# Setup of a fused attention and ternary FFN kernel: k turned, two FFN up blocks, and low parts of weights moved into tile 0

## The reference, cut to what matters

```python
h = x + cosformer_attn(rmsnorm(x, norm1_w), qkv_w, qkv_b, out_w, out_b)   # relu(q), relu(k), causal, 16 heads of 16
return h + gelu(rmsnorm(h, norm2_w) @ mlp_w1 + mlp_b1) @ mlp_w2 + mlp_b2

scale = clip(mean(abs(w_latent), axis=1), 1e-05)                          # bitlinear, for w_fc and w_proj
tern = clip(round(w_latent / scale), -1, 1)
h = bitlinear(x, w_fc) + gate * (x @ v.T @ fast_b.T @ u.T)
return bitlinear(relu(h) ** 2, w_proj)
```

## Time and profile before

| what | value |
|---|---|
| median of three runs | 607.0 us |
| the profiled execution's own time | 607.54 us |
| its span | 605.1 us |
| PE busy | 589.5 us, 97% |
| DVE busy | 395.8 us, 65% |
| ACT busy | 365.1 us, 60% |
| POOL busy | 226.6 us, 37% |

### The profile page before, as it was taken

How to read it: one execution, slowest core, us unless ns; L and a number is a source line. 1 busy time by engine, 2 the same in 40 slices (tenths; PEclk the granted TensorE clock), 3 DMA queues, 4 the chain that set the end, 5 groups by cost and what they waited for, 6 DMA issues and landing times.

```text
span 605.1 us, 14558 instructions
## 1 busy us (share of the span) xinstructions
PE 589.5 (97%) x5162; PEld 525.3 (87%) x5162; DVE 395.8 (65%) x757; ACT 365.1 (60%) x656; POOL 226.6 (37%) x267
## 2 busy tenths in 40 slices
PE   7979999999999999999999999999999999999996
PEld 7868888998898898988899988998989988999785
DVE  6998783685648674585846856486745858457532
ACT  6775774567546765567645675466755676456642
POOL 6446414372144612453142721436124531426220
PEclk9999999999999999999999999999999999999999
DMA  7851026300461007500263004610065002620001
GB/s 222 265 173 53 3 74 115 92 20 2 118 119 42 17 0 155 122 0 17 61 127 89 17 0 117 123 38 17 0 151 127 0 17 54 131 59 2 2 1 35
DMA packets 28009, 42.02 MB, mean 69 GB/s; under 512 B 9024, under 2 KB 19920, under 8 KB 27984
## 3 DMA queue, kind: packets, MB, share of 16 engines
q1 hardware_dynamic: 26800, 39.59, 27.9%
q10 hardware_dynamic: 672, 1.05, 0.6%
q0 software_dynamic: 512, 1.05, 0.6%
HBM read 12.31 MB, written 4.19 MB: 27 GB/s over the span
## 4 chain that ended last, share of the span: by engine, by line
PE 91%; DVE 4%; ACT 3%; issue 1%; POOL 0%; DVEq 0%; POOLq 0%
PE accum L1286 25%; PE dense L1271 10%; PE dense L1454 9%; PE shared L1309 6%; PE ctx_ps L1334 5%; PE dense L1459 5%; PE dense L1321 4%; PE dense L1172 4%; PE shared L1427 3%; PE shared L1186 3%; PE ctx_ps L1345 2%; PE dense L1276 2%; PE dense L1176 2%; PE upd_ps L1359 2%; PE ctx_ps L1203 1%; PE accum L1374 1%
## 5 line engine op out<-in xcount | busy, mean ns | idle before, releaser
L1017 DVE TENSOR_TENSOR wide_lo<-wide,wide_hi 128x512 fp32r<-128x512 f32 x128 | 89.5, 699 | 117.6 <-ACT wide_hi L713 100.4
L1025 DVE TENSOR_TENSOR weighted<-shared,cst 128x512 f32<-128x512 f32 x128 | 82.9, 684 | 18.2 <-PE shared L1309 18.2
L710 ACT ACTIVATE wide<-dense,b 128x512 f32<-128x512 f32 x64 | 44.0, 688 | 83.2 <-PE dense L1459 82.8
L1286 PE MATMUL accum<-w_hi,wide_hi 128*128 128x256 f32 x256 | 72.9, 285 | 2.1 <-DVE wide_lo L1017 2.1
L554 POOL TENSOR_TENSOR state<-state,added 128x544 f32<-128x544 f32 x32 | 43.5, 1359 | 81.1 <-DVE added L1047 80.8
L1286 PE MATMUL accum<-w_lo,wide_hi 128*128 128x256 f32 x256 | 71.9, 281 | 0.0
L1286 PE MATMUL accum<-w_hi,wide_lo 128*128 128x256 f32 x256 | 71.6, 280 | 0.0
L1286 PE MATMUL accum<-prT,wide_hi 128*128 128x256 f32 x256 | 66.8, 289 | 0.6 <-DVE wide_lo L1017 0.6
L1286 PE MATMUL accum<-prT,wide_lo 128*128 128x256 f32 x256 | 65.3, 283 | 0.0
L700 ACT ACTIVATE wide<-dense,scales 128x512 f32<-128x512 f32 x64 | 43.9, 686 | 31.6 <-PE dense L1276 31.3
L571 POOL TENSOR_TENSOR xb<-xb,late 128x512 f32<-128x512 f32 x16 | 20.6, 1290 | 110.5 <-DVE wide_lo L1017 110.5
(11 more groups left out here) (178 smaller groups left out, 1496.1 us busy)
## 6 DMA issues: line engine op xcount, KB each, us to landing
k_stack<-weighted SPq DMA_DIRECT2D x96, 128.0 KB, 2.7
q_stack<-arena SPq DMA_DIRECT2D x176, 64.0 KB, 2.3
xin<-L_attn_x SPq DMA_DIRECT2D x16, 256.0 KB, 2.8
out<-late SPq DMA_DIRECT2D x16, 256.0 KB, 2.2
tab<-trig SPq DMA_DIRECT2D x8, 258.0 KB, 2.7
arena<-L_ffn_w_fc SPq DMA_DIRECT2D x1, 1024.0 KB, 7.6
late<-L_ffn_w_proj SPq DMA_DIRECT2D x1, 1024.0 KB, 7.6
xs<-L_attn_mlp_w SPq DMA_DIRECT2D x2, 512.0 KB, 6.4
```

Source lines behind the costliest of these rows:

```text
L710: act.activation(wide[:, m % 2, :], dense[m % 2][:, :], ACT.Gelu_apprx_tanh, bias=b1[:, m:m + 1]).then_inc(dense_free, 1)
L1017: dve.tensor_tensor(wide_lo[:, n % 2, :], wide[:, n % 2, :], wide_hi[:, n % 2, :].bitcast(F32), ALU.subtract).then_inc(lo_done, 1)
L1025: dve.tensor_tensor(weighted[:, g, :].rearrange("p (a n) -> p a n", a=4), shared[g % 2][:, :].rearrange("p (a n) -> p a n", a=4), mask.rea ...
L1286: mm = pe.matmul(accum[k // 2][:, (k % 2) * E:(k % 2 + 1) * E], a[:, n % 2, tok], w[:, n % HB, :], start=(first and i == 0 and k % 2 == 0) ...
```

## The change

In the setup ACT makes the high parts of k and q as soon as each block is there, and DVE only the low parts; w_fc becomes ternary in two halves, each behind its own scale columns; `wo` is loaded ahead of w_fc and split earlier; ACT instead of DVE makes `diag_scale`. On PE the turn of k, the scale product, FFN up blocks 0 and 1 stand between the turns of u and of w_proj, the latter goes block by block into `accum0`, `accum1`, `ctx_ps` and `upd_ps`, and two of three `keep_busy` are gone. The low parts of w1 and the layernorm go behind the first score groups of tile 0, the w2 quarters to other places in it, and the second half of w1 to the middle of ACT's list. Stacking in tile 0 is issued and waited for by halves (groups 0 and 1, then 2 and 3); POOL starts its part once the high parts of q are there.

The diff, cut:

```diff
-KEEP = (8, 4, 8)
+KEEP = 8
...
+        def wait_k_stack(eng, t, i):
+
+            eng.wait_ge(k_stacked[i], (t + 1) * N_K_STACK // 2 * 16)
+
+        def wait_q_lo(eng, t, i):
+
+            eng.wait_ge(q_lo_stacked[i], (t + 1) * N_Q_LO // 2 * 16)
...
+            sp.dma_start(raw_wo, out_w.rearrange("(k p) n -> p k n", p=P)).then_inc(in_wo, 16)
             sp.dma_start(raw_fc, w_fc.rearrange("(m p) n -> p m n", p=P)).then_inc(in_fc, 16)
-            sp.dma_start(raw_wo, out_w.rearrange("(k p) n -> p k n", p=P)).then_inc(in_wo, 16)
...
-                for g in range(4):
+                def stack_k(g):
                     for slot, part in enumerate((0, 0, 1)):
                         sp.dma_start(k_stack[slot:P:4, g, :, :].bitcast(F32),
-                                     k_parts[32 * g:32 * g + 32, part, :, :]).then_inc(k_stacked, 16)
-                sp.wait_ge(q_parts_done, (t + 1) * 2 * KE)
-                for g in range(4):
-                    stack_q(sp, g, 1, 1, q_lo_stacked)
-                if not isinstance(t, int) or t:
+                                     k_parts[32 * g:32 * g + 32, part, :, :]).then_inc(k_stacked[g // 2], 16)
+
+                if isinstance(t, int) and t == 0:
+                    for i in range(2):
+                        stack_k(2 * i)
+                        stack_k(2 * i + 1)
+                        if i == 0:
+                            sp.wait_ge(q_parts_done, 2 * KE)
+                        stack_q(sp, 2 * i, 1, 1, q_lo_stacked[i])
+                        stack_q(sp, 2 * i + 1, 1, 1, q_lo_stacked[i])
...
-            pool.wait_ge(q_parts_done, 2 * KE)
+            pool.wait_ge(q_hi_made, KE)
...
-                    if isinstance(t, int) and t == 0 and j == 0:
+                    if first and j == 1:
                         pool.wait_ge(in_small, 16 * N_SMALL)
                         pool.wait_ge(w1_lo_done, KE)
-                        pool.wait_ge(lo_done, 2)
                         for g in range(2):
                             x_plus_b2(0, g)
-                    if 1 <= j <= 2:
+                    if first and j >= 2:
+                        xn_plus_ob(j - 1)
+                    elif not first and 1 <= j <= 2:
...
+            def k_hi(m):
+                act.wait_ge(dense_free, m + 1)
+                act.activation(k_parts[:, 0, m, :].bitcast(F32R), kT[:, m, :], ACT.Copy).then_inc(k_hi_made, 1)
+
+            def q_hi(m):
+                act.wait_ge(dense_free, KE + m + 1)
+                act.activation(q_parts[:, 0, m, :].bitcast(F32R), qT[:, m, :], ACT.Copy).then_inc(q_hi_made, 1)
+
+            for m in range(4):
                 sum_abs_fc(m)
             act.wait_ge(in_qkb, 16)
             relu_block(0, 0)
-            for m in range(HB // 2, HB):
-                sum_abs_fc(m)
-            for i in range(1, 2 * KE):
-                relu_block(0, i)
+            k_hi(0)
+            sum_abs_fc(4)
+            sum_abs_fc(5)
+            relu_block(0, 1)
+            k_hi(1)
+            sum_abs_fc(6)
+            sum_abs_fc(7)
+            relu_block(0, 2)
             act.wait_ge(qkv_split, 3 * KE)
-            for m in range(KE):
-                act.wait_ge(dense_free, KE + m + 1)
-                act.activation(q_parts[:, 0, m, :].bitcast(F32R), qT[:, m, :], ACT.Copy).then_inc(q_hi_made, 1)
+            q_hi(0)
+            relu_block(0, 3)
+            q_hi(1)
...
-            act.dma_start(raw_w1[1], mlp_w1[P:2 * P, :]).then_inc(in_w1[1], 16)
-            w1_hi_half(0)
-            read(SET_SC, pr_scale_row[:, :], ctx_ps[:, 0:E])
-            for g in range(4):
-                read(SET_PR + g, prT[:, 2 * g:2 * g + 2, :].rearrange("p h n -> p (h n)"), (accum + dense)[g][:, :])
-            w1_hi_half(1)
-
-            act.wait_ge(set_pe, SET_ALL)
-            act.dma_start(raw_w2[0], mlp_w2[0:4 * P, :].rearrange("(k p) n -> p k n", p=P)).then_inc(in_w2, 16)
+            act.wait_ge(set_dve, N_SET_PR)
+            act.wait_ge(in_const, 16)
+            for m in range(KE):
+                act.activation(diag_scale[:, m, :], ident, ACT.Copy,
+                               scale=scales[:, HB + m:HB + m + 1]).then_inc(diag_done, 1)
...
                 if first:
+                    read_k(0)
+                    read_k(1)
+                    read(SET_SC, pr_scale_row[:, :], ctx_ps[:, 0:E])
+                    act.dma_start(raw_w1[1], mlp_w1[P:2 * P, :]).then_inc(in_w1[1], 16)
+                    w1_hi_half(0)
+                    ffn_block(0)
+                    for g, bank in enumerate((accum[0], accum[1], ctx_ps, upd_ps)):
+                        read(SET_PR + g, prT[:, 2 * g:2 * g + 2, :].rearrange("p h n -> p (h n)"), bank[:, :])
+                    act.dma_start(raw_w2[0], mlp_w2[0:4 * P, :].rearrange("(k p) n -> p k n", p=P)).then_inc(in_w2, 16)
+                    ffn_block(1)
+                    ready_v()
...
+                    if first and j == 0:
+                        w1_hi_half(1)
...
+            split_weight(raw_wo, in_wo, wo_hi, wo_lo, wo_split)
...
-            k_part(0, 0)
-            n = scale_columns(n, 0, HB, E)
-            dve.reciprocal(g_by_s[:, :], scales[:, 0:HB]).then_inc(set_dve, 1)
-            n += 1
-            dve.wait_ge(set_dve, n)
...
+            def fc_half(g, n, between):
+
+                dve.wait_ge(set_dve, n)
+                fc_less(4 * g)
+                for m in range(4 * g, 4 * g + 4):
+                    if m < 4 * g + 3:
+                        fc_less(m + 1)
+                    n += 1
+                    fc_ternary(m, n)
+                    if m == between:
+                        k_low_part(1)
+                return n
+
+            n = scale_columns(n, 0, HB // 2, E)
+            k_low_part(0)
+            n = fc_half(0, n, 1)
+            q_low_part(0)
+            n = scale_columns(n, HB // 2, HB, E)
+            dve.reciprocal(g_by_s[:, :], scales[:, 0:HB]).then_inc(set_dve, 1)
+            n += 1
+            q_low_part(1)
+            n = fc_half(1, n, None)
...
-                dve.tensor_scalar(both, raw_pr[:, m, :], half_neg[:, c:c + 1], None, ALU.is_lt).then_inc(set_dve, 1)
-                dve.tensor_scalar(diag_scale[:, m, :], ident, scales[:, c:c + 1], None, ALU.mult).then_inc(diag_done, 1)
+                dve.tensor_scalar(pr_less, raw_pr[:, m, :], half_neg[:, c:c + 1], None, ALU.is_lt).then_inc(set_dve, 1)
...
-            n = pr_ternary(1, n)
             for g in range(2):
                 dve.wait_ge(read_out, SET_G + g + 1)
                 part = gT[32:64, g * TOK:(g + 1) * TOK]
                 dve.tensor_tensor(part, dense[g][32:64, :], part.bitcast(F32), ALU.subtract).then_inc(g_lo_done, 1)
             z_lo(0)
+            n = pr_ternary(1, n)
...
-            w1_lo_half(0)
-            dve.wait_ge(wo_split, 2)
-            layernorm(0)
-            w1_lo_half(1)
-            dve.wait_ge(read_out, SET_SC + 1)
...
+                first = isinstance(t, int) and t == 0
+                if first:
+                    split(0)
+                for i in range(2):
+                    wait_k_stack(dve, t, i)
                 weigh(0, 0)
-                split(0)
+                if not first:
+                    split(0)
                 weigh(0, 1)
                 for j in range(NB):
                     if j:
                         context(j - 1)
                     weigh(j, 2)
                     weigh(j, 3)
-                    if isinstance(t, int) and t == 0:
-                        w2_quarter((j + 2) % 4, j)
-                    first = isinstance(t, int) and t == 0
+                    if first and j < 2:
+                        w1_lo_half(j)
+                    if first and j == 0:
+                        dve.wait_ge(pr_tern, KE)
...
+                        layernorm(0)
                     if first and j == 2:
+                        w2_quarter(2, 0)
+                        w2_quarter(3, 1)
+                    if first and j == 3:
                         ln_statistics(t + 1, range(2))
-                    if more and j == (3 if first else 0):
+                    if more and j == 0 and not first:
                         sum_halves(t + 1)
                     split(j + 1)
-                    if first and j == 2:
+                    if first and j == 3:
                         ln_statistics(t + 1, range(2, NB))
+                        sum_halves(t + 1)
...
+                if first:
+                    w2_quarter(0, 2)
...
+                if first:
+                    w2_quarter(1, 3)
...
-                keep_busy(KEEP[g])
+                if g == 0:
+                    keep_busy(KEEP)
             pe.wait_ge(u4_done, 1)
-            pe.wait_ge(read_out, SET_FC + 4)
             for g in range(2):
+                pe.wait_ge(read_out, SET_FC + 2 * g + 1)
                 for i in range(4):
                     mm = pe.transpose(dense[g][:, i * P:(i + 1) * P],
```

(46 more changed lines are left out.)

115 lines of the change are left out of this document (63 added, 52 removed).

## The result

The changed kernel takes 610.27 us (median of six runs, 609.58 to 611.94) against 606.65 us for the kernel before in runs beside it. The ratio is 1.0062, 95% interval 1.0045 to 1.0078: it is **slower by 0.6%**, where 602.1 us was forecast, and the range (600.9 to 605.0) missed it. The profiled execution took 610.13 us, its span is 607.7 us, 2.6 more than before.

What follows compares the result with a forecast made beforehand. PE bounds the kernel from tile 1 on, so time saved ahead of the first full chunk is saved at the end. 5.2 gained by chunk 1's group 2, less 0.3, is 4.9; 607.0 - 4.9 = 602.1 us, range 600.9 to 605.0.

Steps and rivals of the forecast that it cites:

- DVE and PE up to the first scores: Setup: u scaled at 25.8 instead of 26.66, first scores at 34.4 instead of 38.60.
- DVE up to the first weigh: Tile 0, chunk 0: DVE free for split at 34.7, weigh follows at 35.3 instead of 40.95.
- The new wait: PE ahead of group 2's scores, for ACT's prT reads and second-half stacks: start at 37.2, bounds 36.6 and 38.7.
- SP issues for the same 13.8: SP's 20 stacking DMAs in tile 0: start 0.3 later, issue for 13.8 us as before, until 33.5.
- The Trainium skill's rule: Stacking DMAs: all issuers share 16 engines, so POOL's earlier start brings no byte forward; sum 4.1 instead of 4.9.
- DVE behind the wait: Chunk 0 from group 2: 7.15 us of DVE work, so chunk 1's group 2 at 44.35, 5.2 us earlier.
- A low clock here is mostly covered: Chunk 0 behind group 2: PE needs 5.3 of the 7.15 and waits for DVE, mostly covering a low clock.
- Chunks 1 to 3: Tile 0: chunk 1's DVE work of 5.6 to 6.0 covered by PE's 5.87; chunk 2's two w2 quarters taken at nothing.
- End of tile 0: A w2 quarter of 1.1 ahead of k and q parts, against DVE's 0.74 idle: PE loses 0.3.
- the first: Rival: second half of the stacks lands late, group 2 at 38.7, 1.5 later: 603.6 us; chance 0.18.
- The second: Rival: ACT becomes the bound, its chain slips by 2.8, prT read at 40: 604.9 us; chance 0.09.
- The third: Rival: PE's clock stays low from group 2 through chunk 1, costing 9.4: 611.5 us; chance 0.06.

Runs made afterwards that it cites:

- 12: Run 9 with low q stacks of groups 2 and 3 on POOL and the last w2 quarter ahead of split 6: 603.64 us, ratio 0.9924 to 0.9962.
- run 10: Run 7 with POOL instead of SP stacking the low parts of q of groups 2 and 3: 605.77 us, ratio 0.9970 to 0.9995.
- run 1: The changed kernel with POOL again waiting for all parts of q before stacking: 609.34 us, ratio 1.0032 to 1.0078.
- run 2: The changed kernel with SP stacking all of k first, then the low parts of q: 609.24 us, ratio 1.0024 to 1.0059.
- run 4: The changed kernel with POOL late, k stacked first and the w2 load held, all together: 610.58 us, ratio 1.0046 to 1.0089.
- 13: Run 11 with SP stacking all of k first, then the low parts of q: 608.01 us, ratio 1.0002 to 1.0030.
- run 11: Run 9 with the last w2 quarter moved ahead of split 6: 604.10 us, ratio 0.9937 to 0.9968.
- 14: Run 11 with POOL waiting for all parts of q before stacking: 604.47 us, ratio 0.9948 to 0.9972.
- run 3: The changed kernel with the load of w2's first half issued behind the v products: 607.60 us, ratio 0.9996 to 1.0024.
- run 5: Run 3 with the load of w1's second half also moved behind the v products: 609.94 us, ratio 1.0036 to 1.0075.
- 8: Run 3 with 24 unread matmuls on PE in its wait for the second half of the stacks: 610.05 us, ratio 1.0035 to 1.0078.
- run 9: Run 7 with 10 unread matmuls on PE in its wait for the stacks: 604.52 us, ratio 0.9947 to 0.9974.
- run 7: Run 3 with POOL's two long operations held until DVE has made both w2 quarters of chunk 2: 606.44 us, ratio 0.9974 to 0.9998.
- run 16: The kernel before with 9 unread matmuls on PE in its wait for the first weigh: 606.86 us, ratio 0.9987 to 1.0012.
- run 6: Run 3 with the two w2 quarters of chunk 2 set one in chunk 2, one in chunk 3: 607.86 us, ratio 1.0001 to 1.0025.

## Why the prediction was wrong, step by step

- *DVE and PE up to the first scores*: right. u at 26.29 (25.8 forecast), the first ternary block at 28.17 (28.0), first scores at 34.49 (34.4). `wo` came in time.
- ***DVE up to the first weigh* failed in its last step.** `split` at 34.95 was as forecast (34.7), but `weigh` did not follow at 35.3: it waited 4.70 us for the stacks of k and started at 40.33. The prediction counted DVE's own work and not the buffer that `weigh` shares with the parts of k. The new order puts the k stacks of groups 2 and 3 behind the low parts of q of groups 0 and 1, and with that this bound alone would have held group 2 back to about 41.2 (an estimate: 40.33 and the 0.8 to 0.9 us by which group 2 follows in runs 12 and 10).
- ***The new wait* failed.** It put group 2 at 37.2, at most 38.7; it started at 41.91, released by the last landing of q, 4.1 later than in the kernel before (37.74 to 41.83).
  1. "SP issues for the same 13.8": 17.9. I carried the sum of a queue over to another order and another neighbour. From 26 to 30 us the engines moved 192 GB/s, 197 with POOL late, 229 with k first, 253 with both and w2 held (runs 1, 2, 4), 265 before. But the landing did not follow these figures: with k first it came 0.4 earlier (run 2) or 1.2 later (13 against 11), with POOL late 0.3 earlier (1) or 0.6 later (14 against 11), all within the scatter. So no run shows what made SP's queue longer.
  2. The w2 load, not in the sum at all: 2.2 us of the landing (run 3), 1.9 over all runs. The prediction counted the 512 KB load that starts later than before, w1, which cost nothing that shows (run 5), and overlooked the one that now starts earlier, at 34.78 instead of 36.27, ahead of the tail and not behind it.
  3. SP starts at 20.21, 0.8 later instead of 0.3.

  The w2 load and the later start are 3.0 of the 4.1 at most; the rest, 1.1 or more, stays open. With the load held, k first and POOL late together (run 4) the landing was still 1.5 behind the kernel before, at a start of SP 0.6 later. In the kernel before the landing (37.74) had 0.9 us to spare ahead of the first scores (38.60), and DVE's work held group 2 back to 41.68 anyway; the change used up both.
- *The Trainium skill's rule*, weighed there, that another issuer brings no byte forward: run 1 agrees, as far as its 0.5 us of POOL's start goes (group 2 0.3 us earlier without the early start, not later). The sum by it, 4.1, missed as mine did, since neither held the w2 load.
- *DVE behind the wait*, 7.15: measured 7.77 at the low clock and 6.29 at the full one (runs 8 and 9). The term that was too large is the layernorm, 1.3 from start to start in the changed kernel (45.79 to 47.08) and not 2.2: before, POOL worked beside it. "A low clock here is mostly covered" was wrong by 1.5 us here, and by 1.1 in run 3 and 2.0 in run 7. What it costs in the kernel before is open (run 16).
- *Chunks 1 to 3*, "taken at nothing": chunk 1 right (5.87 from 49.68 to 55.55), chunk 2 lost 1.56 (a wait of 1.89 instead of 0.33). The durations of the earlier trace rows were taken from a place where POOL was quiet.
- *End of tile 0*, 0.3: 0.26 in PE's wait (0.80 in run 9, 0.54 in run 11), though in the changed kernel itself only 0.06 (0.60 against 0.54). "SP stacks tile 1 by 1.1 later; PE did not wait for that": they start 3.0 later (86.85 against 83.86), and PE did wait, 0.46, by way of the load of x.
- *The rivals*: the first had the place (late stacks, released by a DMA) with a size of 1.5 where it was 4.7. The second did not come: ACT had read `prT` at 36.54. (Its "read at 40" is the start of group 2; 36.5 + 2.8 is 39.3.) The third had the low clock, for 6.8 us and not through chunk 1; its 9.4 us were 1.5. (It would have decided from a quarter of chunk 1 on, 4.9 - 3.5 = 1.4 of 5.9, not from a third.)

What stays open: what makes SP's 20 DMAs take 17.9 us instead of 13.8, and with it 1.1 us or more of the late landing; POOL's start at its old time was not tried. Why one 512 KB load cost about 2 us and the other nothing that shows is open too: that its place right ahead of the tail decides is argued, not shown. The last 0.4 us of the chunk boundary at 72 us (a low part of 1.90 instead of 0.69, beside POOL) was not tried by itself.

## What to carry to other kernels

When a wait that hid a landing is taken away, list every transfer issued before that landing, above all those that now start earlier, and ask of every engine behind it which buffer it needs back from a queue (here `weigh` from the stacks of k). A queue's issuing time belongs to its order and its neighbours: don't carry the sum over. A duration holds for the neighbour that stood beside it: ask what POOL does beside each SBUF operation of DVE. And fill a wait of PE with as many unread matmuls as end ahead of it, no more, and only where PE does not run into a wait for another engine behind it.

## What the runs showed of the hardware that I had not expected

- POOL operations of 1.6 us beside DVE copies of 0.42 stretched them to 0.72 and 1.50, and differences of 0.69 to 1.10; a `split` reached 1.77 (run 6). POOL's residual sum took 1.73 us there, and 1.30 where nothing was stretched beside it. `weigh`, with a PSUM operand, kept its 1.28 for two (run 7).
- The granted clock fell to 0.50 in or just behind idle times of 6.32, 4.09 and 2.44 us of PE, and stayed at 1.00 with 0.99 and 0.55 around ten unread matmuls. Idle times of 1.9 us in chunk 2 went either way: 1.00 behind it in the changed kernel and run 3, 0.50 in run 4 (62.9 to 66.3).
- Four of SP's DMAs moved to POOL made the low parts of q land 2.0 us earlier, while six others on SP took 7.16 us instead of 5.36 to issue (run 10); these landed at about the same time (38.8 against 38.65), though SP began them 0.8 earlier.
